# A two-layer graph network on one core: the first edge loop in 56 fixed blocks of 1792 edges, run as five passes over spans of 128 nodes

## The reference

```
q, k, v = x@Wq, x@Wk, x@Wv
scores  = sum over a head of q[dst] * k[src] / 4
m       = segment_max(scores, dst);  ex = exp(scores - m[dst])
agg     = segment_sum(ex * v[src], dst) / (segment_sum(ex, dst) + 1e-9)
h1      = layernorm(x + agg@W0);  y = layernorm(h1 + relu(h1@fc1 + b)@fc2 + b)
x       = layernorm(x + y)
```

```
h_in/h_out = segment_sum(relu([x[src], edge_attr, req]@W1 + b1)@W2 + b2, dst)
x = layernorm(x + relu(((1+eps)*x + h_in + h_out)@Wu + bu))
```

## Time and profile before

| | |
|---|---|
| median of three runs | 2734.34 us |
| the profiled execution | 2738.81 us, of it 2737.0 us from the first instruction to the last |
| busy | POOL 66%, PE 61%, DVE 55%, ACT 20% |
| granted TensorE clock, mean | 0.775 |
| gathers of 1 KB rows (L581) | 850 |
| gathers of 512 B rows (L629) | 784 |
| moved by DMA | 203.94 MB |

### The profile page before, as it was taken

One profiled execution on the slowest core, in us unless ns is written; L12 is line 12 of the kernel. 1 busy time (PEld: TensorE's weight loads), 2 busy tenths in 40 slices (PEclk: granted clock), 3 DMA queues, 4 the chain that ended last, 5 costly groups with the idle time before them and its releaser, 6 DMA issues.

```text
span 2737.0 us, 36397 instructions
## 1 busy us (share of the span) xinstructions
PE 1670.2 (61%) x9440; PEld 1270.3 (46%) x9441; DVE 1500.4 (55%) x3221; ACT 538.4 (20%) x1401; POOL 1817.3 (66%) x1690
## 2 busy tenths in 40 slices
PE   0535666666666666666647875666666666666665
PEld 0424555555555555555545653444444434444443
DVE  2644666666666666666658972344444444444443
ACT  0431111111111111111112331111111111111111
POOL 1027777777777777777751115777777777777775
PEclk9866777777777777777768996777777777777777
DMA  3414333333333333333310112222222222222221
GB/s 102 154 55 96 96 94 94 94 95 95 95 94 96 95 94 95 96 95 94 96 40 13 37 38 53 57 60 58 60 60 59 59 60 58 59 60 58 59 59 47
DMA packets 161868, 203.94 MB, mean 75 GB/s; under 512 B 77391, under 2 KB 121819, under 8 KB 161711
## 3 DMA queue, kind: packets, MB, share of 16 engines
q0 software_dynamic: 65888, 162.90, 21.6%
q1 hardware_dynamic: 92046, 39.37, 5.7%
q10 hardware_dynamic: 3908, 1.38, 0.2%
HBM read 184.85 MB, written 25.06 MB: 77 GB/s over the span
## 4 chain that ended last, share of the span: by engine, by line
POOL 52%; issue 22%; DMA 12%; DVE 6%; PE 4%; SPq 3%; ACT 1%; DVEq 0%; POOLq 0%; ACTq 0%
POOL arena L581 30%; POOL arena L629 22%; DMA arena<-y_tab,arena 5%; DMA kv_tab<-arena 3%; DMA arena<-i 2%; SPq L349 1%; DVE arena L1513 1%; PE ps L1073 1%; SPq L471 1%; DVE arena L1423 1%; PE ps L1033 1%; DVE arena L1413 1%; DMA keeps<-arena 0%; DMA i<-arena 0%; PE ps L1007 0%
## 5 line engine op out<-in xcount | busy, mean ns | idle before, releaser
L581 POOL DMA_INDIRECT arena<-kv_tab,arena x850 | 936.8, 1102 | 287.5 <-issue 258.6
L629 POOL DMA_INDIRECT arena<-y_tab,arena x784 | 813.1, 1037 | 262.2 <-issue 238.6
L971 PE MATMUL ps<-arena 128*128 x2550 | 268.1, 275 | 287.8 <-ACT arena L740 211.3
L1121 PEld LDWEIGHTS ps<-arena 128*128 128x128 f32 x1568 | 275.2, 256 | 326.7 <-ACT arena L849 275.4
L1121 PE MATMUL ps<-arena 128*128 128x128 f32 x1568 | 306.7, 353 | 158.8 <-ACT arena L849 158.7
L1513 DVE TENSOR_TENSOR arena<-ps,arena 128x512 f32<-128x512 f32 x224 | 139.5, 623 | 453.1 <-DMA arena<-y_tab,arena 453.1
L971 PEld LDWEIGHTS ps<-arena 128*128 128x128 bf16 x2550 | 224.9, 126 | 339.1 <-ACT arena L740 290.5
L849 ACT ACTIVATE arena<-arena 128x512 f32<-128x512 f32 x224 | 129.0, 576 | 864.4 <-DVE arena L1513 864.4
L1007 PEld LDWEIGHTS ps<-arena 128*128 128x128 f32 x1600 | 275.3, 260 | 0.0
L961 PE MATMUL ps<-ident,arena 128*128 128x128 f32 x850 | 159.4, 319 | 189.7 <-DVE arena L1327 189.7
L1007 PE MATMUL ps<-arena 128*128 128x136 f32 x1600 | 273.6, 348 | 0.0
(11 more groups left out here) (242 smaller groups left out, 2163.2 us busy)
## 6 DMA issues: line engine op xcount, KB each, us to landing
arena<-kv_tab,arena POOLq DMA_INDIRECT x850, 2.8
arena<-y_tab,arena POOLq DMA_INDIRECT x784, 2.5
eat<-ea SPq DMA_DIRECT2D x59, 112.0 KB, 2.0
ea<-in_edge_attr_dram SPq DMA_DIRECT2D x2, 3125.0 KB, 22.3
kv_tab<-arena SPq DMA_DIRECT2D x10, 625.0 KB
y_tab<-arena SPq DMA_DIRECT2D x20, 312.5 KB
out_dram<-arena SPq DMA_DIRECT2D x56, 64.0 KB, 1.9
xs<-in_x_dram SPq DMA_DIRECT2D x1, 3125.0 KB
```

What stands on the lines that cost most here:

```text
L581: g.indirect_dma_start(kv_s[:, u, t, :], None, kv_tab, bass.IndirectOffsetOnAxis(ap=v3(idx, 2)[:, u, t:t + 1], axis=0)).then_inc(l_g[u][k] ...
L629: g.indirect_dma_start(yg_s[:, r, t, :], None, y_tab, bass.IndirectOffsetOnAxis(ap=v3(idx1, 2)[:, u, t:t + 1], axis=0)).then_inc(m_g[r][k] ...
L971: last = mm(bank(x_)[:, t * D:(t + 1) * D], st_s[:, x_, t * P:(t + 1) * P], qsp[:, ds(tile + part * D, D)], start=(part == 0), stop=(part ...
L1121: last = mm(bank(6 + u)[:, 0:W], yg_s[:, r, t, :], hot1_s[:, u, t, :], start=(t == 0), stop=(t == G1 - 1))
```

## The change

All edges of the first layer are now cut as the second layer's are: 56 blocks of 1792 edges (14 per partition), each over a span of 128 nodes that starts at the block's first destination. Chunk tables of both layers come from the blocks' first destinations, so the counting goes. The loop runs as a pipeline of five passes over a ring of four blocks (`passes4` with depth 4): block `new` gets its scores, `a_` (one behind) the scans across partitions, `b_` (two behind) the differences, masks, weighting and sums, `c_` (three behind) the division, `e_` (four behind) the copy to `nodes`. Queries are no longer kept in SBUF: they are stored to `q_tab`, and each block loads its 128 rows (`load_queries`). The transposed masks come from a line: SP loads all 1792 destinations of a block, broadcast to 128 partitions (`load_line`, one buffer `dstb`), and ACT turns it into masks with a Square and a Relu (`lane_masks`). PE multiplies them in fp32. The last node of a block is carried to the next by a product with `uc`, added in `averages`. Penalties come from differences of neighbouring destinations, times -1e30 on ACT.

In the preparation a partition holds 50 consecutive nodes, x comes in five transfers on five semaphores, PE takes it without POOL's copy, one matmul of 384 columns makes q, k and v, ACT and DVE take turns to copy it out, and three buffers let stores run behind each other. dst and src are loaded from ACT's queue. The copy of the edge attributes to `ea1` moves behind the first loads of the loop. In the node passes the division, its five transposes and copy are gone; ACT makes `nTa` from `nodes`, and two of the three normalisations are done on ACT (`normalised`) with scales from DVE (`scales`). `yst` has two buffers. The second loop reads `nodes` in place of `xs`.

```diff
+            def store_rows(i):
+                u = i % KVR
+                sp.wait_ge(s_ca, acts(i * GRP + GRP - 1))
+                sp.wait_ge(s_cv, vecs(i * GRP + GRP - 1))
+                sp.dma_start(by_row(kv_tab, i * GRP, GRP), kvst_s[0:NT, u, :, D:QKV]).then_inc(s_kvo[u], 16)
+                sp.dma_start(by_row(q_tab, i * GRP, GRP), kvst_s[0:NT, u, :, 0:D]).then_inc(s_kvo[u], 16)
+            for i in range(GROUPS):
+                store_rows(i)
+                if i == 2:
+                    store_table(0)
+                    sp.wait_ge(s_ea, 16 * 10)
+                    sp.dma_start(firsts[1].rearrange("(b c) -> b c", c=1), marks(d1), allow_slow_non_contiguous=True).then_inc(s_first[1], 16)
+                if i == 3:
+                    load_table(0)
+                    sp.wait_ge(s_first[1], 16)
+                    spread(1)
+                if i == 7:
+                    store_table(1)
+                if i == 8:
+                    load_table(1)
...
+            def load_heads(chunk, r):
+                off = entry0(chunk, 0, NB * CH)
+                sp.dma_start(v3(dcol, RING)[:, r, 0:G], by_lane(d0[ds(off, CH)])).then_inc(l_ld[r], 16)
+                sp.dma_start(v3(dcol, RING)[:, r, G:DC], by_lane(d0[ds(off + G, CH)])[:, 0:2]).then_inc(l_ld[r], 16)
+            def load_line(chunk):
+                off = entry0(chunk, 0, NB * CH)
+                sp.dma_start(dstb, d0[ds(off, DB)].rearrange("(a n) -> a n", a=1).to_broadcast([P, DB])).then_inc(l_db, 16)
+            def load_queries(chunk, u):
+                base = entry0(chunk, 1, N)
+                sp.dma_start(v3(qwin, 2)[:, u, :], q_tab[ds(base, W), :]).then_inc(l_qw[u], 16)
+            def sp_edges(r, new, a_, b_, c_, e_):
+                if new is None:
+                    return
+                u = r % 2
+                if b_ is not None:
+                    sp.wait_ge(s_d0, 48)
+                    sp.wait_ge(l_dcr, picked)
+                load_heads(new + 2, (r + 2) % RING)
+                sp.wait_ge(s_arr, 16 * 3)
+                sp.wait_ge(l_ml, ended)
+                load_index(new + 4, r)
+                sp.wait_ge(s_d0, 48)
+                sp.wait_ge(l_hT, formed)
+                load_line(new + 3)
+                sp.wait_ge(s_arr, 16 * 3)
+                sp.wait_ge(l_q, asked)
+                load_queries(new + 3, 1 - u)
...
+            sp.wait_ge(l_q, BASE + NP_)
+            load_queries(2, 0)
+            for h in range(2):
+                sp.dma_start(ea1[h * BASE1:h * BASE1 + HALF, :].rearrange("(p c) f -> p (c f)", p=EP),
+                             ea[h * HALF:(h + 1) * HALF, :].rearrange("(p c) f -> p (c f)", p=EP)).then_inc(s_eac, 16)
+            passes4(sp, sp_edges, n0, 4)
...
+            def gather_chunk(r):
                 pool.wait_ge(s_init, 3)
+                pool.wait_ge(l_ix[r], landed)
+                pool.wait_ge(l_pvb, slot_free)
+                for k, (s0, n) in enumerate(PIECES):
...
+            def lane_masks(chunk, u, r):
+                act.wait_ge(l_paq, plus2)
+                pq_ = v3(paq, RING)[0:H, r, :]
+                a.activation(pq_, pq_, ACT.Copy, scale=-BIG).then_inc(l_paqc, 1)
+                line = dstb[:, 1:CH + 1]
+                a.activation(line, line, ACT.Square, bias=njc[:, ds(chunk, 1)]).then_inc(l_sq, 1)
+                act.wait_ge(l_sq, plus2)
+                if asked_from(chunk):
+                    act.wait_ge(l_q, asked)
+                a.activation(ucol[:, ds(chunk, 1)], line[:, CH - 1:CH], ACT.Relu, scale=-1.0, bias=1.0)
+                a.activation(hotT.rearrange("n (u g e) -> n u g e", u=2, g=G)[:, u, :, :], line.rearrange("n (e g) -> n g e", g=G),
+                             ACT.Relu, scale=-1.0, bias=1.0).then_inc(l_hT, 1)
+                act.reg_add(plus2, plus2, 1)
...
+            def act_edges(r, new, a_, b_, c_, e_):
+                u = r % 2
+                if b_ is not None:
+                    a.activation(v3(dcr, 2)[:, u, :], v3(dcol, RING)[:, (r + 2) % RING, 1:G + 1], ACT.Identity,
+                                 bias=nj[0][:, ds(b_, 1)]).then_inc(l_dcr, 1)
+                if c_ is not None:
+                    a.activation(uc[:, 1 - u:2 - u], ucol[:, ds(c_, 1)], ACT.Copy)
+                    act.wait_ge(l_agg, minus3)
+                    a.activation(v3(cur, 2)[:, 1 - u, :], bank(5)[:, 0:RW], ACT.Copy).then_inc(l_cur, 1)
+                if e_ is not None:
+                    base = act.value_load(tab_sb[0][0:1, ds(5 * e_ + 1, 1)], min_val=0, max_val=N)
+                    act.wait_ge(l_ra, minus4)
+                    a.activation(nodes[:, ds(base, W)], bank(7)[:, 0:W], ACT.Copy).then_inc(l_avT, 1)
+                if b_ is not None:
+                    act.wait_ge(l_d, minus2)
+                    a.activation(contrib_s[:, u, :, :, DH], dif.rearrange("p (h g) -> p g h", h=H), ACT.Exp)
+                    a.activation(v3(fac, RING)[0:1, (r + 2) % RING, :], dcar[0:1, :], ACT.Exp).then_inc(l_e, 1)
+                if new is not None:
+                    penalties(1 - u, (r + 1) % RING)
+                    lane_masks(new + 2, u, (r + 2) % RING)
...
+            def lanes(r):
+                dve.wait_ge(s_init, 3)
+                dve.wait_ge(l_db, landed_l)
+                line = dstb[0:H, 0:CH].rearrange("h (p g) -> h g p", g=G)
+                more = dstb[0:H, 2:CH + 2].rearrange("h (p g) -> h g p", g=G)
+                pq_ = paq_s[0:H, r, :].rearrange("h (k p) -> h k p", k=2)
+                tt(pq_[:, 0, :], more[:, G - 2, :], line[:, 0, :], ALU.subtract)
+                tt(pq_[:, 1, :], more[:, G - 1, :], line[:, 1, :], ALU.subtract).then_inc(l_paq, 1)
+                dve.reg_add(landed_l, landed_l, 16)
...
+            def local_max(r):
+                fl, pl = mx[0], penl_s[:, r, :]
+                dve.wait_ge(l_penl, now)
+                link(scan(fl, pl[:, 0:HW], sco_s[:, r, :], -BIG, op0=ALU.add, op1=ALU.max))
+                scan(ml_s[:, r, ::-1], pl[:, HW:0:-1], fl[:, ::-1], -BIG, op0=ALU.add, op1=ALU.max).then_inc(l_ml, 1)
...
+            def averages(u, r, c_):
+                sums = cur_s[:, u, :].rearrange("p (h w) -> p h w", h=H)
+                dve.wait_ge(l_cur, minus3)
+                if not (type(c_) is int and c_ == 0):
+                    dve.wait_ge(l_ra, minus4)
+                    dve.wait_ge(l_avT, minus4)
+                    link(stt(ctmp[0:1, :].rearrange("p (h w) -> p h w", h=H), bank(7)[0:1, W:W + RW].rearrange("p (h w) -> p h w", h=H),
+                             hot_s[0:1, u, 0, 0:1], fac_s[0:1, r, :, None].to_broadcast([1, H, AW]), ALU.mult, ALU.mult))
+                    link(tt(cur_s[0:1, u, :], cur_s[0:1, u, :], ctmp[0:1, :], ALU.add))
+                link(ts(rden, sums[:, :, DH], 1e-9, None, ALU.add))
+                link(v.reciprocal(rden, rden))
+                tt(av.rearrange("p (h w) -> p h w", h=H), sums[:, :, 0:DH], rden[:, :, None].to_broadcast([P, H, DH]), ALU.mult).then_inc(l_av, 1)
...
+            def masks(u):
+                dve.wait_ge(l_dcr, minus2)
+                tt(hot_s[:, u, :, :], iota_row[:, None, :].to_broadcast([P, G, P]), dcr_s[:, u, :, None].to_broadcast([P, G, P]),
                    ALU.is_equal).then_inc(l_hot, 1)
...
+            def weighted(u, r):
+                dve.wait_ge(l_e, minus2)
+                for s0, s1, done in ((0, PVA, l_pva), (PVA, G, l_pvb)):
+                    tt(contrib_s[:, u, s0:s1, :, 0:DH], kv_s[:, r, s0:s1, D:2 * D].rearrange("p g (h w) -> p g h w", h=H),
+                       contrib_s[:, u, s0:s1, :, DH:AW].to_broadcast([P, s1 - s0, H, DH]), ALU.mult).then_inc(done, 1)
...
+            def dve_edges(r, new, a_, b_, c_, e_):
+                u = r % 2
+                if new is not None:
+                    scores(r, 0)
+                if b_ is not None:
+                    differences((r + 2) % RING)
+                if new is not None:
+                    scores(r, 1)
+                if a_ is not None:
+                    across((r + 3) % RING)
+                if c_ is not None:
+                    averages(1 - u, (r + 1) % RING, c_)
+                if new is not None:
+                    steps(1 - u, (r + 1) % RING)
+                    lanes((r + 2) % RING)
+                if b_ is not None:
+                    masks(u)
+                    weighted(u, (r + 2) % RING)
+                if new is not None:
+                    scores(r, 2)
+                    scores(r, 3)
+                    local_max(r)
...
+            def normalised(to, t3, norm):
+                for t in range(GRP):
+                    last = a.activation(to[:, t, :], t3[:, t, :], ACT.Identity, scale=norm[3][:, t:t + 1], bias=norm[4][:, t:t + 1])
+                return last
             def act_pass(new, mid, old):
+                if new is not None:
+                    a.activation(v3(nTa, GRP), by_tile(new), ACT.Copy).then_inc(n_aT, 1)
...
```

1123 lines of the change are left out of this document (501 added, 622 removed).

## The result

| | before | changed |
|---|---|---|
| median | 2735.22 us (6 runs, 2734.3 to 2736.6) | 2721.06 us (6 runs, 2716.8 to 2726.9) |
| ratio | 1 | 0.9948, 95% interval 0.9936 to 0.9961 |
| span of the profiled run | 2737.0 | 2714.5 |
| first gather, first loop, rest to the second loop, second loop | 201.1, 1218.4, 244.7, 1072.8 | 169.5, 1216.5, 257.6, 1070.9 |

What follows compares the result with a forecast made beforehand. POOL's gathers and DVE's holds bound both loops. Preparation 140 + copy 5 + first loop 1153.6 + its end 31 + node passes 223 + second loop 1072.8 = 2625.4, adjusted to 2623 us; own range 2590 to 2665, with rivals 2530 to 2690.

Steps and rivals of the forecast that it cites:

- What bounds: Both edge loops: priced by POOL's gathers, one per 1.25 us, POOL waiting for nobody except when long two-SBUF-input DVE operations hold it.
- I take 3.1: First loop: loss per block from one 3.95 us hold by `masks` and `weighted`, giving 20.6 us a block.
- Rival (1): First loop: small stall, POOL gets in at the seams of `masks` and `weighted`; 18.9 us a block, 2528 total, 14%.
- Rival (5): First loop: every two-input DVE operation holds POOL, scans too; 23.1 us a block, 2763 total, 2%.
- PE set the period: Node passes: PE nearly full, 18.1 us a pass against 18.27, saving only 20.5 at the start; stage 244.7 becomes 223.
- Preparation, 140: Time to first gather: transfers of x, indices, kv and q stores added up, plus 3 to begin and 2 for last landing.
- What the prediction wrote of few engines: Preparation: 125 partitions put a transfer on 5 engines, by the skill's rule; DMA shares 0.37 and 0.25 leave most idle.
- rivals (1) and (2): Faster cases, 14% each: POOL let in at first-loop seams, 2528; preparation transfers spread, first gather at 88, 2571.
- rivals (3) to (5): Slower first-loop cases: `load_line` bounds, 3049, 5%; DVE's chain bounds, 2724, 5%; all two-input operations hold POOL, 2763, 2%.
- The line: First loop: `load_line` transfer of 7 us, cycle 16.4 under the block's 20.6, so costing nothing.
- The copy of edge_attr: First loop's start: copy moved there holds DVE some 25 us in its second block; charged 5 (0 to 25).
- rival (4): First loop: DVE's chain with three waits is the bound at 22.4 us a block; 2724 total, 5%.

Runs made afterwards that it cites:

- e8_lanes: Changed kernel with `steps` and `lanes` moved behind `weighted` in the first loop, no wait added; 2639.09 us, ratio 0.9651.
- e5_iota: Changed kernel with the row that `masks` compares with read from PSUM instead of SBUF in the first loop; 2616.02 us, ratio 0.9569.
- e6_psum: e5_iota with the exponentials that `weighted` multiplies by also read from PSUM; 2532.31 us, ratio 0.9263.
- e12_all: Changed kernel with PSUM operands, second-loop masks halved, node-pass normalisations on DVE, `nTa` behind the second relu, preparation transfers cut at partition 112; 2413.13 us, ratio 0.8822.
- e11_poolw: e4_split with all loads of weights issued from POOL's queue instead of ACT's; 2666.75 us, ratio 0.9751.
- e15_order: e12_all with tables and arrays behind the first stores on SP's queue; 3152 us on a slow chip, ratio 0.977.
- e4_split: Changed kernel with each x load and each `kv_tab` and `q_tab` store cut into partitions 0 to 111 and 112 to 124; 2668.97 us, ratio 0.9753.
- e17_early: e12_all with SP's queue reordered, weights on POOL's queue, and POOL released ahead of the loads for the loop; 2432.15 us, ratio 0.8887.
- e18_copylast: e17_early with the copy of the edge attributes issued behind the second table's transfers; 2430.72 us, ratio 0.8892.
- e13 to e16: Slow-chip runs: e8_lanes plus an idle subtraction over 8, then 128 partitions (3188, 3203 us); e12_all with stores first, then also weights on POOL's queue (3152, 3138).

## Why the prediction was wrong, step by step

- **What bounds** was right: both loops at 1.25 us a gather, POOL waiting for nobody, and holds by DVE. 784 gathers, one span a block, the second loop and the end of the first (31 us) came as worked out, and so did PE's load in the first loop, 11.4 us a block for 11.3.
- **"I take 3.1" for the stall** failed, by 0.64 a block, 35 us. The mechanism was right. The run was measured from `masks`; it begins with `lanes`. The earliest held gather started 0.52 us ahead of `masks`. With 4.6 for 3.95 the same formula gives 3.8, and 3.74 was measured. `lanes` had been counted in DVE's load, not in the hold.
- **Rival (1)**, POOL let in at the seams, was held off by "nothing waited between the operations". That reason is not enough: e8_lanes has no wait there and lets POOL in. In the earlier trace rows the two products of one line are held as one, and so they are everywhere; `masks` and `weighted` are another case, and `lanes` decides it. With the seam open the change would have been 82 us faster (e8_lanes).
- **Rival (5)**, two-input operations hold POOL whatever their length, was put at 23.1. They do hold: in e5_iota a gather that meets `lanes` takes 1.12 instead of 0.95. But a hold costs its length less the place in the slot, so four scans of 0.4 cost next to nothing. The sentence of the Trainium skill (GPSIMD Engine Reference, the table ahead of 1.1) on two SBUF inputs is borne out by e6_psum: one input in PSUM, and the stall is gone.
- **Node passes: "PE set the period"** failed, by 4.8 us a pass, 35 us. PE was busy 104 of 128 us in before and that was read as the bound; DVE was busy 117 of the same 128. What set the pass there, no run shows. In the changed kernel it is the chain around the engines, and PE's waits are the places where it passes through the others. The stage's 223 had no range at all. On that chain the change put `nTa`, a normalisation of 2.0 for 1.37, and the other one ahead of `nTx`, and with PE's longer wait came a lower clock. DVE's relief was worth nothing, as the prediction said: with both normalisations back on DVE and `nTa` moved a pass is 18.5 in e12_all, beside 18.27 before.
- **Preparation, 140.** The rate of the stores was right (96 for 93), and that their transfers add up, too. What failed are its two ends, "with 3 to begin and 2 for the last landing". Ahead of the first store the sum had only transfers, 45 us; it lacked SP's waits for landings and its issues (until 56.5) and, beside them, ACT's issues (until 47.2). e11_poolw shows that ACT's alone are not the bound, e15_order that SP's order alone isn't. Behind the last store it lacked 15 us of SP's loads for the loop. What the prediction wrote of few engines is shown by e4_split: the first gather comes 54 us earlier for cutting at partition 112. The Trainium skill (DMA: Bandwidth & Descriptors, "Why a DMA increments its semaphore by 16 and not by 1") gives 5 engines for 125 and 16 for 112; the shares 0.37 and 0.85 agree.
- **The line** was hidden, 5.5 us for 7. **The copy of edge_attr** cost nothing instead of 5: no gap of POOL between gathers of the first loop is longer than 0.32 us. The 25 us that the prediction had as its upper bound were too few for a loop that begins earlier: POOL stands 37.5 us in e17_early and 34.8 in e18_copylast.
- The range: rivals (1) and (2) were given 28% between them, and every mis-sized term was on the slow side, where rivals (3) to (5) had 12%. Issue work and the chain of the node passes had no upper bound in the sum. That 2721 lies 3 us from the price of rival (4) is chance: its mechanism, DVE's waits as the bound of the loop, isn't there.

## What to carry to other kernels

A gather on POOL pays for DVE's runs of operations with two SBUF inputs: price the whole unwaited run, short operations ahead of it too, break it with waits into pieces of about 1 us, or put one operand into PSUM. An engine that is 80% busy and waits a little in each pass need not be the bound: follow the chain round all engines before putting work on the one that "has room". In a preparation, count for each queue what it issues and waits for before its first useful transfer, and look whether the partition count lets a transfer use all engines.

## What the runs showed of the hardware that was not expected

- A seam between two long DVE operations without a wait is open or closed to POOL by what stands ahead: open in 53 of 54 blocks of e8_lanes (the one closed has an 8-partition scan ahead), in 0 of 54 of the changed kernel, closed by one subtraction over 8 partitions x 112 (6 blocks) and not by one over 128 x 112 (5 blocks).
- A gather in the same place takes 4.7 us or 0.95 by the memory of one operand of each long DVE operation (block 21.2 in the changed kernel, 17.6 in e6_psum).
- Two DMA issues on ACT (L695, L697) took 9.8 and 9.7 us each. With x cut at partition 112 (e4_split) the same two took 14.1 and 6.0, 20 us together as before; what they stand for, x or their own transfers, no run shows.
- Between chips: the kernel before took 3221 us on one, 2733 to 2737 on the others; in the traces from there (e13 to e16) DVE stands 455 to 599 us ahead of one copy (L1356), where it waits for nothing elsewhere. The profile names no releaser; that gathers land late there is a guess.
